# A decoder layer in three stages: the feed-forward moved into the block of the two stages before it, its first batches between their last steps

## The reference

```
x = x + rwkv(layernorm(x))            # mix with the token before, r,k,v,g,w projections, a scan, W_o
x = x + cross(layernorm(x), ctx)      # 16 heads of 32 channels, 128 context tokens per batch
x = x + ffn(layernorm(x))             # 512 -> 2048 -> 512, int8-like activations, ternary weights

# cross:
q = hs @ Wq.T + bq ; k = ctx @ Wk.T + bk ; v = ctx @ Wv.T + bv
p = softmax(clip(q k / sqrt(32), -50, 50) with masked tokens at -50)
delta = rs * ((p v) @ Wo.T + bo)      # rs: a scalar clipped to 0..0.3
return layernorm(delta) * gamma + beta
# ffn: per token, quantise layernorm(x) to 8 bits, @ ternary(w1) + b1, exact gelu, again with w2, b2
```

## Time and profile before

| | us |
|---|---|
| median of three runs (1136.87 to 1138.75) | 1137.68 |
| the profiled execution's own time | 1141.61 |
| its span, first to last instruction | 1139.8 |
| RWKV stage | 0 to 637.6 |
| cross stage | 637.6 to 925.6 |
| between, no engine busy | 926 to 937 |
| feed-forward | 937 to 1139.8 |

### The profile page before, as it was taken

The page is one execution under the profiler, slowest core; times in us unless marked ns, Lnnn a source line. Parts: engine busy times, 40 slices in busy tenths (PEclk is TensorE's granted clock), DMA queues, the critical chain, the costliest instruction groups (busy, mean ns, idle before and its releaser), DMA issues. The chain is left out here.

```text
span 1139.8 us, 17405 instructions
## 1 busy us (share of the span) xinstructions
PE 931.8 (82%) x6866; PEld 753.4 (66%) x6866; DVE 802.3 (70%) x1186; ACT 520.3 (46%) x735; POOL 148.5 (13%) x210
## 2 busy tenths in 40 slices
PE   2657898998988899898868799999999414988986
PEld 1547787887878788788768677888777301444442
DVE  4856879687787867778485359877777824777763
ACT  5454352534535254351523134444344203888884
POOL 3001010110201011010101000000000002344341
PEclk9778999899999989999989899999999667999998
DMA  9211011020111102004030321133321012121210
GB/s 258 84 47 34 13 38 56 10 84 10 49 36 38 57 10 65 11 28 149 19 129 1 111 93 34 79 110 110 110 74 66 28 56 59 66 84 56 84 66 28
DMA packets 38117, 72.44 MB, mean 64 GB/s; under 512 B 6484, under 2 KB 7380, under 8 KB 37022
## 3 DMA queue, kind: packets, MB, share of 16 engines
q1 hardware_dynamic: 36926, 68.37, 18.0%
q0 software_dynamic: 1120, 3.10, 1.0%
HBM read 57.84 MB, written 12.58 MB: 62 GB/s over the span
## 5 line engine op out<-in xcount | busy, mean ns | idle before, releaser
L678 PE MATMUL S<-R,K 128*128 128x128 f32 x896 | 119.2, 289 | 41.3 <-DVE K L966 41.3
L678 PEld LDWEIGHTS S<-R,K 128*128 128x128 f32 x896 | 112.9, 201 | 45.8 <-issue 45.6
L963 DVE TENSOR_TENSOR R<-R,D 128x512 f32<-128x512 f32 x96 | 66.7, 695 | 30.9 <-PE S L678 30.9
L1615 DVE TENSOR_SCALAR E<-S,upper 128x2048 f32<-128x2048 f32 x16 | 37.6, 2350 | 52.8 <-PE S L1471 52.6
L1946 PE MATMUL Hp<-wq,xqT 128*128 128x512 bf16 x256 | 68.2, 390 | 7.8 <-DMA w1b<-b1p 4.0
L377 POOL TENSOR_TENSOR sm<-sm,mhalf 128x16 f32<-128x16 f32 x8 | 28.6, 3579 | 326.7 <-DVE sm L1012 326.7
L946 DVE COPY_PREDICATED A<-masks,S 128x1024 f32<-128x1024 int32 x40 | 70.0, 1750 | 0.0
L1954 PE MATMUL O<-wq,hqT 128*128 128x512 bf16 x256 | 61.5, 396 | 3.9 <-ACT hqT L1904 3.9
L2000 DVE TENSOR_REDUCE s<-gc 128x1 f32<-128x2048 f32 x16 | 36.6, 2286 | 32.1 <-ACT gc L1911 32.1
L1621 DVE RECIPROCAL rec<-S 128x512 f32<-128x512 f32 x16 | 53.6, 3352 | 1.5 <-PE S L1486 1.4
L925 DVE TENSOR_TENSOR xf<-X,xx 128x1024 f32<-128x1024 f32 x40 | 48.8, 1221 | 8.0 <-PE X L635 7.3
(11 more groups left out here) (279 smaller groups left out, 2796.9 us busy)
## 6 DMA issues: line engine op xcount, KB each, us to landing
wch<-in_wff SPq DMA_DIRECT2D x32, 256.0 KB, 3.1
cwch<-in_wff SPq DMA_DIRECT2D x8, 1024.0 KB, 6.9
xt<-in_x SPq DMA_DIRECT2D x8, 512.0 KB, 3.9
y<-in_x SPq DMA_DIRECT2D x8, 512.0 KB, 3.6
out<-y SPq DMA_DIRECT2D x8, 512.0 KB, 3.2
cxt<-out SPq DMA_DIRECT2D x8, 512.0 KB, 4.3
ct<-in_ctx SPq DMA_DIRECT2D x8, 512.0 KB, 5.3
cxr<-out SPq DMA_DIRECT2D x8, 512.0 KB, 6.8
```

Of the source, the lines that this page charges most:

```text
L678: mm = pe.matmul(ps[:, b, k, :, :].rearrange("p a t -> p (a t)"), K[:, r % 2, T * g:T * g + T], right_tokens(g, i), start=True, stop=True)
L963: dve.tensor_tensor(right, right, wide(decay.unsqueeze(1).unsqueeze(3), right.shape), ALU.mult).then_inc(R_up, 1)
L1615: dve.tensor_scalar(E[b][:, :, :, :].rearrange("p j k t -> p (j k t)"), S[:, :, :].rearrange("p j n -> p (j n)"), upper[:, bass.ds(q * 2 + ...
```

## The change

Semaphores of the RWKV stage are reset by SP in the middle of the cross stage (83 of them, between steps 3 and 4) and used again by the feed-forward, which now stands in the same block. Its tiles lie on places that are free by then: the RWKV projection weights (W_k, W_r, ...), the split halves, xnT. The core of the diff:

```diff
-        with nc.Block() as block:      # the feed-forward's own block; also clear(nc, semaphores)
+        third = ffn_parts(nc, a, x_out, persist, space, psum, ctx)
 # cross, SP
+        def finish(f, done):
+            for n in range(2, 4):
+                step(*(n - s if n >= s else None for s in range(4)))
+            for semaphore in done:
+                sp.sem_clear(semaphore)
+            with sp.Fori(4, PAIRS) as p:
+                step(*(p - s if s else p for s in range(4)))
+            step(None, PAIRS - 1, PAIRS - 2, PAIRS - 3)
+            sp.wait_ge(v_done, PAIRS)
...
+            f["open"]()                # x of batches 0 and 1, b1, b2
+            step(None, None, PAIRS - 1, PAIRS - 2)
+            f["rows"]()                # the nine rows of w1b
+            step(None, None, None, PAIRS - 1)
             sp.wait_ge(x2_out, 16 * PAIRS)
+            f["rest"]()                # feed-forward steps 2 to 19
 # cross, PE
+            run_to_last(pe, step)
+            step(None, None, PAIRS - 1, PAIRS - 2)
+            step(None, None, None, PAIRS - 1)
...
+            f["step"](1)
+            pe.wait_ge(delta, PAIRS)
+            f["rest"]()
 # cross, ACT
+            copy_delta(PAIRS - 1)
+            f["step"](1)
+            normalize_delta(PAIRS - 1)
+            f["rest"]()
 # cross, DVE
+            run_to_last(dve, step)
+            step(None, None, PAIRS - 1, PAIRS - 2)
+            f["open"]()
+            f["step"](0)
+            last_stats(PAIRS - 1)
+            f["step"](1)
+            last_norm(PAIRS - 1)
+            last_gain(PAIRS - 1)
+            add_last(PAIRS - 1)
+            f["rest"]()
 # the context arrives transposed, no turn_ctx; ct is read from SBUF
-        "ctx": np.asarray(inputs["ctx_2048"]),
+        "ctx": np.asarray(inputs["ctx_2048"]).reshape(PAIRS, 2, T, NC, P).transpose(0, 4, 3, 1, 2),
-            act.activation(flat(cs[0]), PFb[:, :], ACT.Copy).then_inc(ch_ready, 1)
+            act.activation(flat(cs[0]), flat(ct), ACT.Copy).then_inc(ch_ready, 1)
 # v without its bias; b_o + b_v W_o is worked out once
-            add_row(PFa[:, C * b:C * b + C], 0)
+        def project_bv():
+            pe.wait_ge(bv_wide, 2)
+            pe.wait_ge(wload["o"], 16)
+            for k in range(NC):
+                mm = pe.matmul(S[0:2 * XD, 3, :], bvw[:, k, :], chunks(stage["o"])[:, k, :], start=k == 0, stop=k == NC - 1)
+            mm.then_inc(bv_done, 1)
 # RWKV, `last` step: PE
-                x["turn_ctx"](0)
                 x["sum_weights"]()
+                x["project_bv"]()
                 x["v_rows"](0, 0)
...
                 x["v_rows"](0, 1)
+                x["turn_x"](1)
 # ACT
+                x["high_ctx"](0)
+                x["high_x"](0)
                 act.wait_ge(v_done, PAIRS)
                 x["split_weight"]("v")
-                x["high_ctx"](0)
-                x["high_x"](0)
...
+                x["high_x"](1)
                 x["copy_v"](0)
+                x["high_ctx"](1)
+                x["bias_high"]()
-        act.wait_ge(x1_out, 16 * PAIRS)
-        x["run"]()
+        x["run"](ffn)
```

More of the change, by code:

```diff
@@ L100, in sem, with kept @@
         return semaphores[-1]
+    def kept(name):
+        return late.enter_context(nc.semaphore("r_" + name))
     R = sb("R", [P, 2, 2 * NC, T])
@@ L1400, in copy_v, with copy_delta, normalize_delta @@
             act.activation(flat(V), PFa[:, :], ACT.Copy).then_inc(v_ready, 1)
+        def copy_delta(r):
+            act.wait_ge(out_done, r + 1)
+            if reached(r, 1):
+                act.wait_ge(x2_ready, r)
+            act.activation(d[:, :, :], S[:, 0:2, :], ACT.Copy).then_inc(delta, 1)
+        def normalize_delta(r):
+            act.wait_ge(d_shifted, r + 1)
+            for b in range(2):
+                act.activation(d[:, b, :], d[:, b, :], ACT.Identity, bias=shd[:, b:b + 1], scale=rsd[:, b:b + 1]).then_inc(d_norm, 1)
         def step(n, p, q, r):
-            if p is not None:
+            if p is not None and reached(p, 2):
                 high_ctx(p)
@@ L1413, in step @@
             if r is not None:
-                act.wait_ge(d_shifted, r + 1)
-                for b in range(2):
-                    act.activation(d[:, b, :], d[:, b, :], ACT.Identity, bias=shd[:, b:b + 1], scale=rsd[:, b:b + 1]).then_inc(d_norm, 1)
+                normalize_delta(r)
             if q is not None:
@@ new lines, in rest @@
+        def rest(f):
+            dve.wait_ge(setup, 8)
+            run_to_last(dve, step)
+            step(None, None, PAIRS - 1, PAIRS - 2)
+            f["open"]()
+            f["step"](0)
+            last_stats(PAIRS - 1)
+            f["step"](1)
+            last_norm(PAIRS - 1)
+            last_gain(PAIRS - 1)
+            add_last(PAIRS - 1)
+            f["rest"]()
+        return {"clear": wipe, "bounds": bounds, "sum_bias": sum_bias, "lower_bias": lower_bias, "prepare": prepare, "split_weight": split_weight, "norm": norm, "norm_shift": norm_shift,
+                "low_ctx": lambda p: low(p, cs, flat(ct), ch_ready, cl_ready), "low_x": lambda p: low(p, xs, PFb[:, :], xh_ready, xl_ready), "run": rest}
@@ L2050, in decoder_layer @@
     with ExitStack() as ctx:
-        psum = {"X0": ctx.enter_context(nc.psum_tensor("X0", [P, 2 * C], F32)), "X1": ctx.enter_context(nc.psum_tensor("X1", [P, 2 * C], F32)),
-                "S": ctx.enter_context(nc.psum_tensor("S4", [P, 4, C], F32))}
-        semaphores = []
-        first = rwkv_parts(nc, a, out, persist, space, psum, ctx, semaphores)
-        second, persist["wq"] = cross_parts(nc, a, out, persist, space, psum, ctx, semaphores)
+        projections = ctx.enter_context(nc.psum_tensor("P4", [P, 4, C], F32))
+        psum = {"F": projections, "S": ctx.enter_context(nc.psum_tensor("S4", [P, 4, C], F32))}
+        for n, at in (("X0", 0), ("X1", 2)):
+            psum[n] = projections[:, at:at + 2, :].rearrange("p j c -> p (j c)")
+        with ExitStack() as early:
+            early_semaphores = []
+            first = rwkv_parts(nc, a, out, persist, space, psum, early, ctx, early_semaphores)
+            second, persist["wq"] = cross_parts(nc, a, out, persist, space, psum, ctx, [])
+        third = ffn_parts(nc, a, out, persist, space, psum, ctx)
         with nc.Block() as block:
```

751 lines of the change are left out of this document (384 added, 367 removed).

## The result

| | before | after |
|---|---|---|
| median of runs | 1137.72 us (4 runs) | 1089.98 us (4 runs: 1088.25, 1088.36, 1091.6, 1092.08) |
| profiled execution: own time, span | 1141.61, 1139.8 us | 1091.6, 1089.8 us |
| ratio, 95% interval | | 0.9581 [0.9557, 0.9604] |

The kernel is 4.2% faster; 1086.6 was forecast with 1076 to 1098 around it. The profiled span falls by 50.0 us, and fixed points in both traces divide that as follows.

A forecast was written before the change was run, and what follows sets the result against it. TensorE was taken to bound the cross period, DVE the last RWKV step, with an idle passage to the feed-forward; -16.1 - 9.5 - 25.5 = -51.1 us took the median from 1137.68 to 1086.6, range 1076 to 1098.

The forecast's parts named there:

- Term 1: Last RWKV step to the cross stage's first clip: shorter levels, added bias work, earlier clip and better clock, -16.1 us.
- the -8.4: Last RWKV step: the 4.04 us wait for `cch` goes and weight splits move behind the levels, saving 4.4 more.
- the -1 of the clock: Last RWKV step: a denser TensorE should lift its granted clock of 0.85 a little, -1 us (0 to -3).
- Rival C: Last RWKV step: half-clock TensorE limits the levels, so the 8.4 us are not gained; 1095 us, chance 0.10.
- The +2.0 behind y: Last RWKV step: `project_bv` ahead of v and the turns of y adds 2.0 us to the path (0.4 to 3.2).
- the 3.67 one: Last RWKV step: DVE's 3.67 us wait for POOL's powers, said to take in one of the moved weight splits.
- Term 2: Cross stage: less TensorE work per step, periods near 32.4 us, -7.5 over five and -2 in the first, -9.5 us.
- `col` bound: Cross loop: DVE's low half of the attention's output then sets the period at 32.4 us, -1.5 per period.
- Rival A: Cross stage: the period does not shorten because clips and `col` hang on PE and ACT; 1094 us, chance 0.08.
- rival D: Cross stage: slow semaphore resets, 17 us together, make pair 4's x late, +5 to 12 us once; chance 0.05.
- Term 3: Passage from cross to feed-forward: first batches interleaved with the last cross steps, batch 2's load gating the first reduction, -25.5 us.
- Rival E: Cross steps: TensorE, waiting a little for DVE, runs at the low clock and the kernel gets slower; chance 0.01.

The follow-up runs named there:

- quantize_late: Changed kernel with DVE's quantising of the feed-forward's weights moved behind the low halves, ahead of the next pair's clip; 1085.52 us, ratio 0.9546 to the kernel before.
- early_load: Changed kernel with SyncE issuing batch 2's load behind the rows of w1b, ahead of the cross stage's last write; 1080.27 us, ratio 0.9499 to the kernel before.
- front_first: Changed kernel with batch 1's front moved ahead of the last pair's statistics on DVE and POOL; 1087.17 us, ratio 0.9546 to the kernel before.
- again: The changed kernel run again without any edit, beside the kernel before; 1087.37 us, ratio 0.9566 to the kernel before.
- split_o_late: Changed kernel with DVE's last-step split of W_o moved from the wait for POOL's powers to that for the output projection; 1088.9 us, ratio 0.9577 to the kernel before.

## Why the prediction was right

**What bounds.** As read: TensorE set the cross period and `col` stood 1.7 us behind (TensorE's own period after the change was put at 31.6 and is 31.51 in quantize_late); DVE carried the last RWKV step; the boundary was idle.

**Term 1**, -16.1 and measured -16.1 (or -14.7 with the other clock), but with parts that are not all what the text said. The levels fell by 8.9 us and the wait behind them by 0.8, together -9.7 for the -8.4 and the -1 of the clock, which the traces don't part. Rival C falls with that. The clip follows the sum by 2.98 us, 2.7 forecast, at the full clock. The +2.0 behind y is right as a number and incomplete as a cause: `project_bv` took 3.65 us (3.5 forecast), but the split of W_o, placed under POOL's power and charged nothing, costs the same 2 us over again, hidden only by `project_bv`. The sentence that puts one split in the wait for y and "the other in the 3.67 one" is what missed: it looked at DVE's idleness, not at the engine that DVE idled for.

**Term 2**, -9.5 and measured -11.8. The `col` bound was the right mechanism: 32.2 to 32.3 for 32.4. That gave 8.7 over the five periods for 7.5; the rest is the first period, -3.1 for -2. Rival A falls. The resets (rival D) took 4.4 us and hid, as charged.

**Term 3**, -25.5 and measured -27.5. The load of batch 2 was the gate, shown by early_load. `front(1)` costs the last sum 2.45 us (front_first; 2.6 forecast). Against pair 6's clip the sum is only 0.8 later in the profile after and 2.0 in "again"; the two differ in how long the last output projection took (statistics 31.48 and 32.73 us behind pair 7's clip). That is the clock: between 24 and 28 us behind the clip TensorE is busy all the time in both and is granted 0.81 in the one and 0.50 in the other. In the profile before it was 0.50 too, so at like clock the sum is 2.0 us later, near the forecast's 2.6. From the sum it is 8.94 us and not 9.7: the write landed after 2.8, not 3.3. The first step of the feed-forward is 0.9 longer than before and not 0.3.

**What no term had** is the +5.4 us ahead of the last step. "again" shows them to be TensorE's clock; the forecast compared one profiled execution with another as if both had the same clock history. It took back what terms 2 and 3 gave beyond the forecast (4.3 us), which is why 1088.7 for the span came out at 1089.8: that this is so near is luck. The profile of "again" has a span of 1085.4 us, 3.3 below the forecast, and its median of 1087.37 is within 1 us of the 1086.6.

**Rival E** falls: TensorE now waits 0.69 us in the cross periods and is granted 1.00 in the window of 733.80 to 766.10 above. The rule of the Trainium skill that was weighed there (TensorE: Matmul & The Clock Gate, "A second HAM failure mode: psum-queue depth-cycling") is not borne out here at a wait of this size. Low stretches lie elsewhere: in the last RWKV step of the profile after TensorE waits 2.95 us for DVE ahead of the level at 586.39, and is granted 0.68 from 585 to 590; such stretches move from run to run.

## What to carry to other kernels

When two stages are merged, look for the next instruction in the queue of whoever issues the loads: here the gate behind the merged boundary was one load, queued behind a write that it did not need, and moving it gave another 5.4 us.

The time in which an engine waits is not free for work that slows the engine it waits for. And where two costs end at the same instant, taking away one shows nothing: remove both before calling either free.

When the bound of a loop moves by 1.6 us and the next engine stands 0.7 behind, move work on that engine too: the same 3.6 us of DVE work, put behind the loop's critical value, gave 0.77 per period.

## What the runs showed that I had not expected

POOL's power of 128x16 numbers takes 2.90 us with DVE idle, 4.87 us when DVE's 128x2048 subtraction of 2.28 us with both inputs in SBUF starts just ahead of it (split_o_late against the changed kernel), and 3.81 us in the RWKV steps in which a 128x1024 one of 1.22 us does. The surplus, 1.97 and 0.91, is nearly what was left of the subtraction when the power started: 2.11 us (613.03 to 615.14) and, in the step of pair 5, 1.05 (489.80 to 490.85). The Trainium skill says in SBUF — State Buffer, "Who interferes with whom", that a DVE instruction with two SBUF inputs contends with a GpSimd instruction that reads SBUF, and calls the shared ports an exclusive lock. The trace agrees, and the page would have warned of the moved split ahead of time.

TensorE's low stretches don't keep their place between runs of one kernel: between 545 and 550 us the clock was 0.58 in one execution (29 matmuls) and 1.00 in another (43). In the 5 us ahead TensorE had been busy for 3.85 us in the profile after, whose clock then fell, and for 3.87 in the profile before, whose clock stayed at 1.00 until 580. Five runs of one kernel lay at 1087.2 to 1087.4 and 1089.7 to 1090.1. Effects under 3 us are read from distances in the trace, at the same granted clock, and not from medians of five.
